# Edge gathers without a loop and with four steps of rows, and sixteen experts without a loop and with five homes of raw weights

## The chip, the cores and the metric

The kernel runs on one core of one Trainium2 chip. The metric is the time of one execution on the device in microseconds (us), the median of three runs. A core has a matrix engine (TensorE, PE in the profile, with its weight loads as PEld), a vector engine (VectorE, DVE), a scalar engine (ScalarE, ACT), a general engine (GpSimd, POOL) that also issues the indirect transfers, and a queue for plain transfers (SyncE, SP). Each engine works through its own list of instructions in order. They meet at semaphores alone, which every transfer and many instructions raise.

## The reference

One layer of a graph network and one layer of experts, over 1250 nodes of 512 values.

```python
xn   = layernorm(x)                                   # 1250 x 512
msg  = relu(xn[src] + edge_attr @ W_e + b_e)          # 21250 edges, sorted by dst
aggr = segment_sum(msg, dst)
h    = silu(bn(((1 + eps) * xn + aggr) @ W1 + b1))    # 1250 x 1024
x    = x + silu(bn(h @ W2 + b2))
t    = layernorm(x)
aff  = softmax(t @ gate_weight)                       # 1250 x 16
gating, index = top_k(aff.T, 156)                     # 156 tokens for each of 16 experts
for e in range(16):
    h = gelu(t[index[e]] @ w1[e] + b1[e])             # 512 x 512 weights
    y = h @ w2[e] + b2[e]
    out[index[e]] += gating[e] * y
out = x + out
```

## The kernel before, in words

Products run in fp16 with each fp32 operand split into a high and a low part, so a product is three matmuls (high by high, high by low, low by high).

**Edges.** The 21250 edges are 34 steps of 5 groups (`J = 5`) of 125 edges. POOL fetches for each group the 125 rows of `node_rows` that `src` names, by one indirect transfer (L413). The rows of a step stand in one of two halves of `rows`, a ring of two steps. Ahead of every second step POOL copies the indices of two steps into `src_now` (L403) and waits for that copy, and ahead of each transfer it waits until PE (`msg_ps`), or for the middle group `Z = 2` DVE (`rowsz_used`), has used the row that stood in its place. PE multiplies the edge attributes (L1165, L1167), adds the fetched rows by two matmuls with a scaled identity (L1182, L1184), and sums the messages of the step before into windows of nodes (L1158). ACT takes the relu (L541) and DVE its low part (L845). For the middle group DVE adds row and product itself (L841). Each engine runs through `run_steps`: a loop of eight turns of four steps, then two steps.

**Middle.** The two node products, their normalisations, the layer norm, the logits, a search for the 156th affinity of each expert (L1000 to L1013), and the places of the chosen tokens (`slot`).

**Experts.** For each expert DVE compares slots (`choose`, ten instructions, L1041), PE turns that into token numbers and gates (`pick_tokens`, L1332), DVE writes `idx` (`indices`, L1056), and POOL gathers 2 x 78 rows of `token_rows` (L426). PE turns the rows (`turn_rows`, L1345), multiplies by w1 (`up`, two halves) and w2 (`down`), both L1202, and turns the result back (`turn_back`, L1380). DVE and ACT weigh it (`weigh`, L1076, L673), and POOL adds the rows to `out` by indirect transfers (L435), each expert's after the last one's have landed (`scatter_end`). The fp32 weights of an expert, 2 x 1024 KB, are loaded by SP into `raw[b]`, two homes, when DVE has finished the low part (L930) of the expert that stood there; ACT makes the high part (L579). Within expert e the engines also work ahead: `pick_tokens`, `indices` and `gather` of expert e+2, `choose` of e+3. PE's order is

```python
up(e, 0); turn_back(e-1); up(e, 1); pick_tokens(e+2); turn_rows(e+1); down(e)
```

DVE's is `expert_low(e+1, 0)`, `weigh(e-1)`, `low_h(e)` (both halves), `columns(e+1)`, `indices(e+2)`, `expert_low(e+1, 1)`, `choose(e+3)`, and POOL's is `scatter(e-1)`, `gather(e+2)`, `scatter_end(e-1)`. The experts run as one, then a loop of three turns of four, then three.

Of the kernel before, what the change touches and what calls it, by code (L numbers as in the profile page):

```python
# [18 lines left out]
def gnn_ffn_kernel(nc, x, src, dst, edge_attr, W_e, b_e, W1, b1, g1, beta1, W2, b2, g2, beta2, eps,  # L19
# [31 lines left out]
    CREDIT = 3 * JP  # L51
# [16 lines left out]
    with ExitStack() as ctx:  # L68
# [12 lines left out]

        def rank(j):

            return j - (j > Z)


        xs = sb("xs", [P, NT, H], F32)
# [9 lines left out]
        We32 = sb("We32", [128, H], F32)  # L97
        We_hi = sb("We_hi", [128, H], F16)
        We_lo = sb("We_lo", [128, H], F16)
        be = sb("be", [P, H], F32)  # L100
        edge = [sb(f"edge{b}", [P, J, ED], F32) for b in range(2)]
        edge_hl = [sb(f"edge_hl{b}", [P, J, 2, ED], F16) for b in range(2)]
        edge_T = [sb(f"edge_T{b}", [128, J, 128], F16) for b in range(2)]
        onehot = [sb(f"onehot{b}", [P, J, WIN], F16) for b in range(2)]
        rel = [sb(f"rel{b}", [P, J], F32) for b in range(2)]
        src_i = sb("src_i", [P, SB, J], I32)
        src_now = [sb(f"src_now{i}", [P, 2, J], I32) for i in range(3)]
        dst_f = sb("dst_f", [P, SB, J], F32)
        dst_left = sb("dst_left", [P, SB, J], F32)
        outside = sb("outside", [P, SB, J], F32)  # L110
# [66 lines left out]
        idx = [sb(f"idx{b}", [KH, 2], U32) for b in range(4)]  # L177
        gat = [sb(f"gat{b}", [KH, 2], F32) for b in range(4)]
# [7 lines left out]
        rows = big[0:P, 0:half].bitcast(F16).rearrange("p (s w h) -> p s w h", w=2, h=H)  # L186
        msg = big[0:P, half:2 * half].bitcast(F16).rearrange("p (s w h) -> p s w h", w=2, h=H)
        rows32 = [big[0:P, (b * J + Z) * H:(b * J + Z + 1) * H] for b in range(2)]
# [10 lines left out]
        pick, xg, xT, hT, h32, yT, yw = [], [], [], [], [], [], []  # L199
        for b in range(2):  # L200
            pick.append(take(P, NT * K // 2).bitcast(F16).rearrange("p (t k) -> p t k", t=NT))
            xg.append(take(KH, 2 * H).bitcast(F16).rearrange("p (a h) -> p a h", a=2))
            xT.append(take(128, HK * K).bitcast(F16).rearrange("p (w k c) -> p w k c", w=2, k=HK))
            hT.append(take(128, HK * K).bitcast(F16).rearrange("p (w k c) -> p w k c", w=2, k=HK))
            h32.append(take(128, HK * K).rearrange("p (k c) -> p k c", k=HK))
        for b in range(2):
            yT.append(z2T[:, b, 0:HK * K].rearrange("p (k c) -> p k c", k=HK))
            yw.append(z2T[0:KH, 2 + b, 0:2 * H].rearrange("p (a h) -> p a h", a=2))
        assert NT == 2 * J and o <= 4 * J * H and HK * K <= N and 2 * H <= N
# [14 lines left out]
        e_raw = [raw[b][:] for b in range(2)]  # L224
# [11 lines left out]

        b1c, g1c, be1c = (colA[:, i * F1:(i + 1) * F1] for i in range(3))
# [8 lines left out]
        xt_ps = sem("xt_ps"); xt_sb = sem("xt_sb"); eps_ready = sem("eps_ready"); pad_clear = sem("pad_clear")  # L246
# [5 lines left out]
        row_in = [sem(f"row_in{i}") for i in range(2 * J)]  # L252
        edge_hi = sem("edge_hi"); edge_lo = sem("edge_lo"); edge_tr = sem("edge_tr"); edge_cp = sem("edge_cp")
        msg_ps = sem("msg_ps"); prod_z = sem("prod_z"); sumz = sem("sumz"); rowsz_used = sem("rowsz_used"); tab32_out = sem("tab32_out"); msg_hi = sem("msg_hi"); msg_lo = sem("msg_lo"); folded = sem("folded")
        rel_ready = sem("rel_ready"); hot_ready = sem("hot_ready"); acc_done = sem("acc_done")
        src_ready = sem("src_ready"); pool_turn = sem("pool_turn"); agg_ready = sem("agg_ready")
# [10 lines left out]
        taken_ps = sem("taken_ps"); slot_ready = sem("slot_ready")  # L267
        pick_ready = sem("pick_ready"); pick_ps = sem("pick_ps"); idx_ready = sem("idx_ready")
        xg_in = [sem(f"xg_in{b}") for b in range(2)]
        ew_in = [[sem(f"ew_in{b}{m}") for m in range(2)] for b in range(2)]  # L270
# [13 lines left out]
        def _(sp):  # L284
# [56 lines left out]
            for b, split in ((0, W1_lo), (1, W2_lo)):  # L341
                sp.wait_ge(split, HK if b == 0 else F1)
                for m, w in enumerate((fw1_t, fw2_t)):
                    sp.dma_start(e_raw[b][:, m, :].rearrange("p (k f) -> p k f", k=HK), w[b]
                                 ).then_inc(ew_in[b][m], 16)
# [5 lines left out]
            for g in range(NT // XG):  # L351
                sp.wait_ge(x16_lo, (g + 1) * XG)
                for r0, r1 in SPRAY:
                    sp.dma_start(rows16_t(token_rows)[r0:r1, g * XG:(g + 1) * XG, :],
                                 x16[r0:r1, g * XG:(g + 1) * XG, :, :].rearrange("p t w h -> p t (w h)")
                                 ).then_inc(rows_out, 16)

            with sp.Fori(0, EX // 2 - 1) as q:
                for b in range(2):
                    for m, w in enumerate((fw1_t, fw2_t)):  # L360
                        sp.wait_ge(e_lo, (q * 2 + b) * 2 + (m + 1))
                        sp.dma_start(e_raw[b][:, m, :].rearrange("p (k f) -> p k f", k=HK),
                                     w[bass.ds(q * 2 + (b + 2), 1)].rearrange("a p k f -> (a p) k f")
                                     ).then_inc(ew_in[b][m], 16)
# [3 lines left out]
        def _(pool):  # L368
# [27 lines left out]
            def step(w, g, b, place):  # L396
                n = w * SB + (g * 2 + b)
                if b == 0:

                    pool.wait_ge(msg_ps, n * JP + JP)  # L400
                    pool.wait_ge(rowsz_used, n + 1)
# [3 lines left out]
                for j in range(J):  # L405
                    if j == Z:
                        pool.wait_ge(rowsz_used, n + 2)
                    else:
                        pool.wait_ge(msg_ps, n * JP + JP + rank(j) + 1)
                    pool.sem_inc(pool_turn, 1)  # L410
                    to, table = (rows32[b], node_rows32) if j == Z else (
                        rows[:, b * J + j, :, :].rearrange("p w h -> p (w h)"), node_rows)
                    pool.indirect_dma_start(to, None, table,  # L413
                                            bass.IndirectOffsetOnAxis(src_now[place][:, b, j:j + 1], 0)
                                            ).then_inc(row_in[b * J + j], 16)

            run_steps(pool, n_pass, SB, step)

            def gather(e):
                b = e[1] % 2  # L420
                pool.wait_ge(idx_ready, num(e) + 1)
                if num(e, least=0) >= 2:
                    pool.wait_ge(xT_ps, num(e) * 2 - 2)
                pool.sem_inc(pool_turn, 1)
                for a in range(2):
                    pool.indirect_dma_start(xg[b][:, a, :], None, token_rows,  # L426
# [12 lines left out]
            def scatter_end(e):  # L439

                pool.wait_ge(y_out[e[1] % 2], pair(e) * 32 + 32)
                pool.sem_inc(scattered, 1)
# [1019 lines left out]
```

## Time and profile before

| what | value |
|---|---|
| median of three runs | 761.31 us (760.77 to 762.72) |
| profiled execution, its own time | 758.0 us |
| its span, from first to last instruction | 756.2 us |
| mean granted TensorE clock | 0.888 of full speed |
| busy: PE, PEld | 530.1, 382.1 us |
| busy: DVE, ACT, POOL | 478.9, 357.5, 360.1 us |
| moved by transfers | 111.34 MB, mean 147 GB/s |

Busy time counts an engine as at work, whatever it waited for in between. The same mean hides stages with different limits, so the stages have to be read one by one: up to 52 us the tables of rows, to 331 us the edges, to 541 us the middle, to 742 us the experts, then the last scatter.

### The profile page before, as it was taken

Reading aid. Unit: us, or ns where it says so; the run is one execution under the profiler, and the core shown is the slowest. Engines: PE = TensorE matmul, PEld = TensorE weight load, DVE = VectorE, ACT = ScalarE, POOL = GpSimd, SP = SyncE. Lnnn points to the kernel's source line nnn. Section 1 sums busy time; section 2 is a strip of 40 time slices with the busy share of each in tenths; the row PEclk is TensorE's granted clock in tenths of the full one; section 3 lists DMA queues with packets and bytes.
Section 4 is the critical chain, followed back from the end, with each engine's and each line's share of the span. In section 5 each row is a group of like instructions: output and inputs, shape, how many; then the busy total and the mean of one; then the engine's idle time right before and its main releaser. Section 6 shows DMA issues by size and latency. Waiting matters only on the chain.

```text
span 756.2 us, 15773 instructions
## 1 busy us (share of the span) xinstructions
PE 530.1 (70%) x5273; PEld 382.1 (51%) x5273; DVE 478.9 (63%) x1042; ACT 357.5 (47%) x610; POOL 360.1 (48%) x284
## 2 busy tenths in 40 slices
PE   1527868788787777769988995712577866968791
PEld 1314445454454444445544554511577866958781
DVE  4944657586666666666539657777566665857650
ACT  0603545355444445454437406530267656756661
POOL 1717777777777777740000000130266456545552
PEclk9999989899989999999998997755589878889996
DMA  7376787868777686643300004150358678688632
GB/s 182 120 215 190 196 197 183 203 180 200 197 182 201 175 203 175 172 115 113 112 0 1 1 0 136 56 182 11 90 148 259 170 212 225 173 218 212 200 52 34
DMA packets 79647, 111.34 MB, mean 147 GB/s; under 512 B 32207, under 2 KB 40842, under 8 KB 79615
## 3 DMA queue, kind: packets, MB, share of 16 engines
q0 software_dynamic: 43712, 53.95, 29.6%
q1 hardware_dynamic: 34637, 56.16, 25.2%
q10 hardware_dynamic: 1266, 0.81, 0.5%
q8 instruction: 19, 0.31, 0.2%
q14 instruction: 13, 0.11, 0.0%
HBM read 95.35 MB, written 15.35 MB: 146 GB/s over the span
## 4 chain that ended last, share of the span: by engine, by line
PE 28%; DMA 19%; issue 17%; POOL 16%; DVE 11%; ACT 5%; POOLq 1%; SPq 0%; ACTq 0%; DVEq 0%
PE bank L1202 16%; POOL big L413 11%; DMA big<-node_rows,src_now 9%; DMA big<-token_rows,idx 6%; POOL out L435 3%; PE bank L1218 2%; POOL big L426 2%; PE bank L1182 2%; DVE stats L699 2%; DMA pair<-in_src 1%; DMA out<-rows_z,idx 1%; PE bank L1345 1%; DVE rows_z L710 1%; PE bank L1184 1%; ACT pair L579 1%
## 5 line engine op out<-in xcount | busy, mean ns | idle before, releaser
L413 POOL DMA_INDIRECT big<-node_rows,src_now x170 | 211.2, 1242 | 63.6 <-issue 43.8
L1202 PE MATMUL bank<-big,pair 128*128 128x156 f16 (+2 forms) x1824 | 177.3, 261 | 7.2 <-DVE big L912 5.3
L1202 PEld LDWEIGHTS bank<-big,pair 128*128 128x128 f16 x1824 | 147.9, 104 | 32.9 <-issue 6.7
L541 ACT ACTIVATE big<-bank 125x512 f16<-125x512 f32 x136 | 81.2, 597 | 127.1 <-PE bank L1184 126.6
L845 DVE SCALAR_TENSOR_TENSOR big<-bank,big 125x512 f16<-125x512 f32 x136 | 90.3, 686 | 41.8 <-ACT big L541 39.0
L1182 PE MATMUL bank<-big,ident_scaled 125*125 125x512 f16 x136 | 59.3, 436 | 71.4 <-DMA big<-node_rows,src_now 70.6
L435 POOL DMA_INDIRECT out<-rows_z,idx x32 | 60.0, 1874 | 61.1 <-ACT rows_z L673 38.2
L426 POOL DMA_INDIRECT big<-token_rows,idx x32 | 55.6, 1738 | 68.3 <-DVE idx L1056 51.9
L454 POOL TENSOR_TENSOR big<-aggT,big 125x512 f16<-125x512 f32 x10 | 11.3, 1155 | 159.3 <-ACT big L602 159.3
L1158 PEld LDWEIGHTS bank<-onehot,big 125*128 125x128 f16 x1400 | 62.5, 101 | 31.9 <-issue 7.5
L1182 PEld LDWEIGHTS bank<-big,ident_scaled 125*125 125x125 f16 x136 | 19.0, 140 | 117.3 <-DMA big<-node_rows,src_now 113.6
L930 DVE SCALAR_TENSOR_TENSOR pair<-raw,pair 128x2048 f16<-128x2048 f32 x32 | 72.9, 2279 | 0.0
L1165 PE MATMUL bank<-We_hi,edge_T 128*125 128x512 f16 x170 | 70.4, 414 | 1.5 <-ACT edge_T L519 1.5
L1167 PE MATMUL bank<-We_lo,edge_T 128*125 128x512 f16 x170 | 67.2, 395 | 0.0
L1158 PE MATMUL bank<-onehot,big 125*128 125x64 f16 x1400 | 66.0, 197 | 1.3 <-DVE big L845 1.3
L579 ACT ACTIVATE pair<-raw 128x2048 f16<-128x2048 f32 x32 | 60.9, 1905 | 0.2
L841 DVE SCALAR_TENSOR_TENSOR big<-big,bank 125x512 f32<-125x512 f32 x34 | 23.3, 686 | 55.6 <-DMA big<-node_rows,src_now 55.6
L1184 PE MATMUL bank<-big,ident_scaled 125*125 125x512 f16 x136 | 54.6, 401 | 0.0
L634 ACT ACTIVATE big<-bank 128x624 f16<-128x624 f16 x16 | 11.1, 692 | 88.1 <-PE bank L1345 87.8
L1345 PE MATMUL bank<-ident,big 78*128 78x78 f16 x256 | 15.5, 232 | 45.4 <-DMA big<-token_rows,idx 45.4
L1345 PEld LDWEIGHTS bank<-ident,big 78*128 78x128 f16 x256 | 13.2, 119 | 46.6 <-DMA big<-token_rows,idx 46.6
L1202 PE MATMUL bank<-rows_z,pair 128*128 128x418 f16 (+1 forms) x192 | 33.9, 338 | 0.0
(197 smaller groups left out, 864.5 us busy)
## 6 DMA issues: line engine op xcount, KB each, us to landing
raw<-in_L_ffn_w SPq DMA_DIRECT2D x32, 1024.0 KB, 6.4
edge<-in_edge_attr SPq DMA_DIRECT2D x35, 140.0 KB
node_rows<-big SPq DMA_DIRECT2D x10, 448.0 KB
raw<-in_L_gnn_W SPq DMA_DIRECT2D x16, 256.0 KB, 7.2
big<-node_rows,src_now POOLq DMA_INDIRECT x170, 5.9
xs<-in_x SPq DMA_DIRECT2D x5, 448.0 KB
out<-xs SPq DMA_DIRECT2D x5, 448.0 KB
token_rows<-big SPq DMA_DIRECT2D x5, 448.0 KB
```

The costliest lines, as they stand in the source:

```text
L413: pool.indirect_dma_start(to, None, table, bass.IndirectOffsetOnAxis(src_now[place][:, b, j:j + 1], 0)).then_inc(row_in[b * J + j], 16)
L426: pool.indirect_dma_start(xg[b][:, a, :], None, token_rows, bass.IndirectOffsetOnAxis(idx[e[1] % 4][:, a:a + 1], 0)).then_inc(xg_in[b], 16)
L435: pool.indirect_dma_start(out, bass.IndirectOffsetOnAxis(idx[e[1] % 4][:, a:a + 1], 0), yw[e[1] % 2][:, a, :], None, compute_op=ALU.add).t ...
L541: act.activation(msg[:, b * J + j, 0, :], rows32[b] if j == Z else bank[j][0:P, :], ACT.Relu).then_inc(msg_hi, 1)
L579: act.activation(pair16[b][:, 0, m, :], raw[b][:, m, :], ACT.Copy, scale=W_SCALE).then_inc(e_hi, 1)
L845: dve.scalar_tensor_tensor(out=msg[:, b * J + j, 1, :], in0=rows32[b] if j == Z else bank[j][0:P, :], scalar=0.0, in1=msg[:, b * J + j, 0, ...
L930: dve.scalar_tensor_tensor(out=pair16[b][:, 1, m, :], in0=raw[b][:, m, :], scalar=W_SCALE, in1=pair16[b][:, 0, m, :], op0=ALU.mult, op1=AL ...
L1158: last = pe.matmul(bank[6 + b][:, k * WIN:(k + 1) * WIN], msg[:, b * J + j, p, k * 128:(k + 1) * 128], onehot[b][:, j, :], start=(j == p = ...
L1165: pe.matmul(bank[j][0:P, :], edge_T[b][:, j, 0:P], We_hi[:], start=True, stop=False, skip_group_check=True)
L1167: return pe.matmul(bank[j][0:P, :], edge_T[b][:, j, 0:P], We_lo[:], start=False, stop=(j == Z), skip_group_check=True)
L1182: pe.matmul(bank[j][0:P, :], ident_scaled[0:P, 0:P], rows[:, b * J + j, 0, :], start=False, stop=False, skip_group_check=True)
L1202: last = pe.matmul(bk, weights(i, k), values(j, k), start=(begin and p == k == 0), stop=(end and p == 2 and k == n - 1), skip_group_check= ...
```

## The change

The edge gathers become straight code, 34 steps with fixed places, a ring of four steps (two in `rows`, two in the room of `pair16`, idle until then), indices read straight from `src_i`, and one pair of waits for each step instead of one for each transfer. Groups 0 and 1 share a semaphore, and so do 3 and 4; the waits for them want both rows. The transposes of the edge attributes move from group 3 to group 1, their copy from group 4 to group 3. The experts become straight code on all engines, with `idx` and `gat` kept for all sixteen, four homes of gathered rows, three of weighed results, and five of raw weights: two as before, and `edge_home`, `xs_home` and `aggT`, which are free at different times. SP loads experts 0, 2, 1 and 5 before the layer's output is stored, 3 and 4 around the storing of the tokens, and the rest as homes come free. `pick_tokens`, `indices` and `gather` work three experts ahead, `choose` four.

```diff
+    RING = 4
+    CREDIT = RING * JP
+    XR = 4
+    YR = 3
+    RH = 5
...
+        def trio(j):
+            return (j >= Z) + (j > Z)
+        def rows_landed(w, g, r, place, n):
+            return w * (16 * n * (SB // RING + (r < SB % RING))) + (g * (8 * n) + n * (16 - 8 * (place % 2)))
...
+        late_rows = [pair16[i][0:P].rearrange("p w a (s h) -> p (w a s) h", h=H)
+                     .rearrange("p (s w) h -> p s w h", w=2) for i in range(2)]
+        def row(r, j):
+            return rows[:, r * J + j, :, :] if r < 2 else late_rows[r - 2][:, j, :, :]
...
+            sp.wait_ge(W1_lo, HK)
+            for m in range(2):
+                load_expert(0, m)
+            sp.wait_ge(agg_ready, 1)
+            for m in range(2):
+                load_expert(2, m)
+            sp.wait_ge(W2_lo, F1)
+            for m in range(2):
+                load_expert(1, m)
+            reload(5)
...
+            for t in range(0, 4, XG):
+                store_tokens(t, XG)
+            sp.wait_ge(x2_out, 16 * NT)
+            sp.wait_ge(xn2_ready, NT)
+            for m in range(2):
+                load_expert(3, m)
+            for t in range(4, NT, XG):
+                store_tokens(t, XG)
+            sp.wait_ge(xt2_ps, NT)
+            for m in range(2):
+                load_expert(4, m)
+            for e in range(6, EX):
+                reload(e)
...
-                    pool.tensor_copy(src_now[place][:], src_i[:, bass.ds(g * 2, 2), :]).then_inc(src_ready, 1)
-                    pool.wait_ge(src_ready, w * (SB // 2) + g + 1)
...
+            with pool.Fori(0, n_pass) as w:
+                for i in range(SB):
+                    ago = RING if i >= SB % RING else SB % RING
+                    pool.wait_ge(msg_ps, w * (SB * JP) + (CREDIT + (i - ago + 1) * JP))
+                    pool.wait_ge(rowsz_used, w * SB + (RING + i - ago + 1))
+                    pool.sem_inc(pool_turn, 1)
+                    for j in range(J):
+                        pool.indirect_dma_start(row32(i % RING) if j == Z else
+                                                row(i % RING, j).rearrange("p w h -> p (w h)"), None,
+                                                node_rows32 if j == Z else node_rows,
+                                                bass.IndirectOffsetOnAxis(src_i[:, i, j:j + 1], 0)
+                                                ).then_inc(row_in[i % RING][trio(j)], 16)
...
+            for e in range(XR - 1):
+                gather(e)
+            for e in range(EX):
+                if e + XR - 1 < EX:
+                    gather(e + XR - 1)
+                if e >= 2:
+                    scatter_end(e - 2)
+                if e >= 1:
+                    scatter(e - 1)
...
+                if e + 1 < EX:
+                    expert_low(e + 1, 0)
+                if e + 3 < EX:
+                    indices(e + 3)
+                low_h(e, 0)
+                if e >= 1:
+                    weigh(e - 1)
+                if e + 1 < EX:
+                    expert_low(e + 1, 1)
+                low_h(e, 1)
+                if e + 1 < EX:
+                    columns(e + 1)
+                if e + 4 < EX:
+                    choose(e + 4)
...
+                pe.wait_ge(idx_ready, min(e + 3, EX))
...
+                up(e, 0)
+                if e + 3 < EX:
+                    pick_tokens(e + 3)
+                if e >= 1:
+                    turn_back(e - 1)
+                up(e, 1)
+                if e + 1 < EX:
+                    turn_rows(e + 1)
+                down(e)
```

## Rows read from the trace of the kernel before

**Rows 1.** Busy us (instructions) by stage: PE, PEld, DVE, ACT, POOL, PEclk, DMA share, GB/s.

```profile
52.00:331.00 279.00, 209.95 (x2091) 126.92 (x2091) 177.20 (x364) 132.27 (x233) 215.73 (x186) 0.95 0.74 187
331.00:541.00 210.00, 145.27 (x931) 88.11 (x931) 140.38 (x335) 82.21 (x129) 16.09 (x14) 0.82 0.18 60
541.00:742.00 201.00, 157.20 (x2187) 155.09 (x2184) 125.44 (x266) 127.76 (x221) 107.83 (x58) 0.87 0.69 183
```

**Rows 2.** The page: the chain that ended last, by line, and two of the costliest groups.

```profile
PE bank L1202 16%; POOL big L413 11%; DMA big<-node_rows,src_now 9%; DMA big<-token_rows,idx 6%; POOL out L435 3%; PE bank L1218 2%; POOL big L426 2%; PE bank L1182 2%; DVE stats L699 2%; DMA pair<-in_src 1%; DMA out<-rows_z,idx 1%; PE bank L1345 1%; DVE rows_z L710 1%; PE bank L1184 1%; ACT pair L579 1%
...
L413 POOL DMA_INDIRECT big<-node_rows,src_now x170 | 211.2, 1242 | 63.6 <-issue 43.8
...
L1345 PE MATMUL bank<-ident,big 78*128 78x78 f16 x256 | 15.5, 232 | 45.4 <-DMA big<-token_rows,idx 45.4
```

**Rows 3.** Timeline of POOL among the edge gathers; the copies over the whole run.

```profile
51.31 0.19 POOL L403 COPY src_now<-src_i 125x10 int32 x1 [15.32 <-issue]
52.64 1.42 POOL L413 DMA_INDIRECT big<-node_rows,src_now  x1 [1.14 <-issue]
...
101.59 1.22 POOL L413 DMA_INDIRECT big<-node_rows,src_now  x1 [0.98 <-PE bank L1184]
103.12 1.21 POOL L413 DMA_INDIRECT big<-node_rows,src_now  x1 [0.31 <-issue]
...
L403 POOL COPY src_now<-src_i x17: 190/208/542, 51.3 to 314.6; 125x10 int32 x16, 125x10 int32<-125x10 int32 x1
```

**Rows 4.** Timeline of DVE: the same instruction of two successive edge steps.

```profile
152.01 0.22 DVE L825 TENSOR_SCALAR rel<-dst_f,shift 125x5 f32 x1
...
157.53 0.49 DVE L825 TENSOR_SCALAR rel<-dst_f,shift 125x5 f32 x1
```

**Rows 5.** Timeline of PE over two experts, and the same products in the straight code near the end.

```profile
600.42 0.73 PE L1345 MATMUL bank<-ident,big 78*128 78x78 f16 x16 [0.37 <-DMA big<-token_rows,idx]
600.99 5.09 PE L1202 MATMUL bank<-big,pair 128*128 128x156 f16 x72
605.92 1.04 PE L1380 MATMUL bank<-ident,rows_z 128*78 128x128 f32 x8
608.44 0.88 PE L1332 MATMUL bank<-tok_aff,big 125*78 x20
615.13 1.22 PE L1345 MATMUL bank<-ident,big 78*128 78x78 f16 x16 [5.80 <-DMA big<-token_rows,idx]
616.15 7.45 PE L1202 MATMUL bank<-big,pair 128*128 128x156 f16 x72
...
727.49 5.09 PE L1202 MATMUL bank<-big,pair 128*128 128x156 f16 x72
```

**Rows 6.** Timeline of POOL and of DVE's L930 in the first of these experts.

```profile
600.22 1.51 POOL L435 DMA_INDIRECT out<-rows_z,idx  x1 [5.54 <-ACT rows_z L673]
601.71 2.28 DVE L930 SCALAR_TENSOR_TENSOR pair<-raw,pair 128x2048 f16<-128x2048 f32 x1
602.03 3.31 POOL L435 DMA_INDIRECT out<-rows_z,idx  x1 [0.30 <-DVE idx L1056]
605.61 2.28 DVE L930 SCALAR_TENSOR_TENSOR pair<-raw,pair 128x2048 f16<-128x2048 f32 x1
605.65 3.12 POOL L426 DMA_INDIRECT big<-token_rows,idx  x1 [0.30 <-issue]
...
609.08 0.99 POOL L426 DMA_INDIRECT big<-token_rows,idx  x1 [0.30 <-issue]
```

**Rows 7.** The chain that ended last, in order of time: start us, us, what.

```profile
729.05 6.28 DMA out<-rows_z,idx
...
738.06 4.24 DMA out<-rows_z,idx
...
743.27 1.47 POOL out L435
```

**Rows 8.** Transfers by issue: count, KB each, median us to landing.

```profile
raw<-in_L_ffn_w SPq DMA_DIRECT2D x32, 1024.0 KB, 6.4
```

More of the change, by code:

```diff
@@ L439, in scatter_end @@
             def scatter_end(e):
-                pool.wait_ge(y_out[e[1] % 2], pair(e) * 32 + 32)
+                pool.wait_ge(y_out[e % 2], e // 2 * 32 + 32)
                 pool.sem_inc(scattered, 1)
-            def expert(e, first=False, ahead=3):
-                if not first:
-                    scatter(after(e, -1))
-                if ahead >= 2:
-                    gather(after(e, 2))
-                if not first:
-                    scatter_end(after(e, -1))
             for t in range(NT):
@@ L683, in _ @@
+            act.wait_ge(z2_ps, 3 * HK)
+            expert_high(1, 0)
+            columns(0)
+            for e in range(EX):
+                expert(e)
+            weigh(EX - 1)
         @block.vector
@@ L1094, in _, with low_h @@
[L1094 to L1102 removed]
+            def low_h(e, half):
+                b, f = e % 2, slice(half * 2, half * 2 + 2)
+                dve.wait_ge(h_high, e * 2 + half + 1)
+                dve.tensor_tensor(hT[b][:, 1, f, :], h32[b][:, f, :], hT[b][:, 0, f, :],
+                                  ALU.subtract).then_inc(h_sb, 1)
@@ L1105, in _ @@
+            dve.wait_ge(rows_out, 16 * NT)
+            choose(0)
+            choose(1)
+            for e in range(3):
+                indices(e)
+                if e < 2:
+                    choose(e + 2)
+            columns(0)
+            for e in range(EX):
+                expert(e)
+            weigh(EX - 1)
         @block.tensor
@@ new lines, in down @@
+                pe.wait_ge(e_lo, e * 2 + 2)
+                if e >= 1:
+                    pe.wait_ge(yT_sb, e * HK)
+                for half in range(2):
+                    pe.wait_ge(h_sb, e * 2 + half + 1)
+                    for d in range(HK):
+                        last = product(bank[4 + d // 2][:, d % 2 * K:(d % 2 + 1) * K], 2,
+                                       lambda i, k: e16[b][:, i, 1, half * 2 + k, d * 128:(d + 1) * 128],
+                                       lambda j, k: hT[b][:, j, half * 2 + k, :],
+                                       begin=(half == 0 and d % 2 == 0), end=(half == 1))
+                        if half == 1:
+                            last.then_inc(yT_ps, 1)
@@ L1393, in expert @@
                 down(e)
-            pick_tokens((0, 0))
-            pick_tokens((0, 1))
-            turn_rows((0, 0))
-            run_experts(pe, expert)
-            turn_back((0, EX - 1))
-def num(e, least=None):
-    q, c = e
-    if least is not None and not isinstance(q, int):
-        return 4 * least + c
-    return q * 4 + c
-def pair(e):
-    q, c = e
-    return q * 2 + c // 2
-def after(e, n):
-    return (e[0], e[1] + n)
+            for e in range(3):
+                pick_tokens(e)
@@ L1420, in run_steps @@
+            turn_rows(0)
+            for e in range(EX):
+                expert(e)
+            turn_back(EX - 1)
 def run_steps(eng, n_pass, steps, step, turn=None, turn_end=None):
@@ L1431, in run_steps @@
             step(w, steps // 2 - 1, b, 2)
-def run_experts(eng, expert):
-    expert((0, 0), first=True)
-    with eng.Fori(0, 3) as q:
-        for c in range(1, 5):
-            expert((q, c))
-    expert((0, 13), ahead=2)
-    expert((0, 14), ahead=1)
-    expert((0, 15), ahead=0)
 def kernel(**inputs):
```

402 lines of the change are left out of this document (168 added, 234 removed).

## The prediction

> **What bounds the kernel now.** I read the chain that ended last first. Apart from PE's products it names POOL's edge gathers, 11%, and the landing of two kinds of gathered rows, 9% and 6% [rows 2]. No engine is full on average, so I cut the span into stages [rows 1]. There are three: the edges, 279 us, with POOL busiest (215.7 us); the middle, 210 us, with transfers at a share of 0.18; and the experts, 201 us, with PE busiest at 157.2 us and its granted clock down at 0.87.
>
> The timeline of POOL shows that it sets the pace of the edges. An edge gather takes 1.24 us on average [rows 2], the next starts 0.30 us later, and that gap does not grow where a semaphore has to be awaited [rows 3]. So 170 gathers want 170 x 1.242 + 169 x 0.305 = 262.7 us, and the stage takes some 278 (52.6 to 331). What is left is the copy of indices. The other engines keep up: DVE begins successive steps 5.5 us apart where the rows are there [rows 4], against 5 x 1.55 = 7.7 us that POOL needs for a step. PE's waits for gathered rows in this stage are POOL's pace seen from behind.
>
> In the experts PE runs one expert in 8.9 us when nothing is late: it starts to turn rows at 600.42 and ends picking at 608.44 + 0.88 = 609.32 [rows 5]. Then it waits 5.80 us for the next gathered rows, and after that wait the same 72 products take 7.45 instead of 5.09 us [rows 5]. Such waits sum to 45.4 us over the run [rows 2]. A row of this stage thus has two costs, the wait and the slow products behind it. The stage's mean is 201/16 = 12.6 us an expert [rows 1].
>
> **The change part by part, edges.** (a) The first copy goes: the copy starts at 51.31, the first gather at 52.64 [rows 3], so -1.3 us. (b) Each of 16 later copies (median 0.21 us) stands with its wait of 0.98 us where otherwise 0.30 us stand [rows 3]: 16 x 0.89 = -14.2. These are POOL's own time, and POOL is the pace, so they come off whole. (c) The ring of four costs or gains nothing in the sum: POOL waits no longer for a place now. It would only pay if the landing time were the pace. The waits moved to the step's head, the later rows in `pair16` and the moved transposes are covered by the 2.2 us a step in which PE and DVE wait for POOL; without that cover, a step is 5.5 us, still below 7.7. (d) The shared semaphores let PE begin group 3 only when group 4 has landed. Within the stage the 2.2 us cover it; at the end one more group of a step comes after the last landing, 5.5/5 = +1.1. Edges together: -14.4.
>
> **Middle.** The loads of experts 2, 5, 3 and 4, 8 MB, run where the transfers' share is 0.18 [rows 1]; a piece of 1 MB lands in 6.4 us [rows 8], and the stage is 210 us long. So 0. If a load stood before the storing of tokens for long, the gather of expert 0 would be late; there are tens of us of search between, so I keep nothing of it. Two more `choose` and a third `pick_tokens` before the first rows are turned: the gather of expert 0 lands meanwhile, but its descriptors are made while DVE is busier. An operation of POOL can stretch from 1.5 to 3.3 us there [rows 6]; between 0 and +2 I take +1.
>
> **Experts.** Gathers are issued two experts or more before PE turns their rows, some 15 us and more against one of 9 us now, so the 5.8 us wait goes, and the slow products with it. What is late next? The bounds of an expert's period:
>
> - Below: PE's 8.9 us [rows 5]. DVE's and ACT's busy time, 125.4/16 = 7.8 and 127.8/16 = 8.0 us [rows 1], leave it room, though `low_h(e, 1)` now stands behind a 2.28 us L930, which can hold `down` for about 0.5 us.
> - Above: POOL. The four transfers of an expert took 600.22 to 610.07 = 9.85 us in one go, two of them stretched from 1.5 and 1.0 to 3.3 and 3.1 us. Each stretched one starts while L930 runs and ends 1 to 1.4 us after it [rows 6]. L930 runs twice per expert, near half of a shorter period, so a third can be hit: 9.85 + 1.8 = 11.6 us. The chain of scatters gives the same size: an issue with its gap, 1.8 or 3.6, a landing of 6.3 and a wake of 1.0 make 9.1 to 10.9 us [rows 7].
>
> I take 9.8 us, the measured POOL sequence, since it is the one resource that already shows this length. With 2 us for the last turning back and weighing the stage is 16 x 9.8 + 2 = 159 against 201: -42. The five homes give their part only here: with two, a period of 9.8 would have to hold two loads and two conversions of the same home; with five, a load has some four periods against 2 x 6.4 us [rows 8].
>
> The row says that POOL stalls behind L930. The Trainium skill, "SBUF — State Buffer", section "Who interferes with whom", says that a DVE instruction with two SBUF inputs contends with a GpSimd instruction that reads SBUF, and that the loser blocks fully; L930 reads `raw` and `pair16`, and the trace agrees (3.31 against 1.51 us). By that rule every transfer that starts inside L930 loses the rest of its 2.28 us, and all four hit would make 6.2 + 4 x 2 = 14 us an expert; it speaks against counting on PE's 8.9.
>
> **Tail.** At the end scatter stands behind scatter: the last begins at 743.27, after the landing of the one before, and 13 us remain from it to the end of the span [rows 7]. That stays. POOL may now be part of an expert behind PE when PE ends, between 0 and 5 us; I take +2.
>
> **Sum.** -14.4 + 0 + 1 - 42 + 2 = -53.4 us from the profiled execution's 758.0 (span 756.2, 1.8 around it): 704.6. The median of the runs is 3.3 above that execution, so 708.
>
> **Rivals.**
>
> - *POOL and the scatters set 11.6 us.* For it: L930 stretches transfers [rows 6], and gathers, scatters and their landing follow each other in POOL's list. Against: two of four transfers were hit, not three. Experts 16 x 11.6 + 2 = 188, 29 us more than forecast: 737.
> - *PE sets 8.9 us.* For it: a whole expert ran so [rows 5]. Against: POOL's 9.85. 14 us less: 694, and with no lag at the end 691.
> - *The edges gain nothing*, because the landing or DVE's wait for the middle row, not POOL's issue, is the pace. Against: the gaps of 0.30 [rows 3]. Experts as forecast: 708 + 15 = 723.
> - *The wait for rows stays*, since `indices` of the third expert ahead, POOL's list or full transfer queues make gathers as late as now. A period of 9.8 moves 2.74 MB (two weight pieces and four times 78 rows of 2 KB), 280 GB/s, against 183/0.69 = 265 at full share [rows 1]. For it: ten experts' loads then fill the queues. Against: four homes in hand. Only the edges gain: 761 - 14 = 747. The Trainium skill, "SBUF — State Buffer", section "A bandwidth-pool intuition that's wrong", gives 358 GB/s between HBM and a core, by which the queues would not fill; 265 is what I reckon with.
> - *Slower: the engines wait for their own instructions.* Without loops each expert's code is new. If PE lost a landing of 6.4 us [rows 8] per expert on that, the period is 8.9 + 6.4 = 15.3, the stage 247, the time 761 - 11 + 46 = 796. It decides from (201 - 2 + 11)/16 = 13.1 us, that is from 4.2 us an expert. Against: the last three experts are straight code already, and their 72 products take the same 5.09 us [rows 5].
>
> **How the numbers follow.** Forecast, a period of 9.3 to 10.5 us (700 to 720): 0.50. POOL near 11.6: 0.17. PE near 8.9: 0.15. Edges without gain: 0.10. Wait for rows stays: 0.05. Slower: 0.03. The range runs from the PE case, 691, to just short of 11.6 us, 734; it leaves out most of the last two cases and the outer half of the POOL case. Within 0.3%, 2.3 us, a measurement of this kernel can tell nothing; the cases put 0.01 there, 0.96 on faster and 0.03 on slower.
>
> **What the profile after would show.** Edges: no copy, one gather each 1.55 us without a break, the stage some 263 us long. Experts: no wait of PE for `token_rows` after the first; a period near 9.8 us with POOL nearly gapless, its transfers of 3 us beside L930; clock above 0.87. Loads of six experts before 541 us. The prediction is wrong if PE's wait for rows is still there, if POOL's gap in the edges was something else than the copy, or if POOL's transfers stretch further than two in four.

## The result, and the profile after

The changed kernel took 736.44 us (median of 4, 733.0 to 738.94) against 761.22 us of the kernel before (760.77 to 762.72): a ratio of 0.967, 95% interval 0.962 to 0.972. That is a gain of 25 us, somewhat less than half of the 53 forecast, and the time lies outside the range of 691 to 734 us. The profiled execution took 733.0 us, its span is 731.2 us.

I cut its span as before: at 331 us, where the edges ended then, and where PE first turns gathered rows and ends its last turning back. In the windows view the columns are those of [rows 1].

```profile
52.00:331.00 279.00, 215.77 (x2102) 142.28 (x2103) 178.19 (x365) 129.41 (x233) 209.16 (x170) 0.93 0.79 190
331.00:538.00 207.00, 144.64 (x940) 88.42 (x937) 141.59 (x346) 82.12 (x128) 16.14 (x15) 0.83 0.26 89
538.00:704.00 166.00, 145.74 (x2175) 141.78 (x2172) 122.93 (x253) 126.33 (x221) 120.94 (x54) 0.97 0.68 181
704.00:731.00 27.00, 0.00 (x0) 0.00 (x0) 0.28 (x1) 0.63 (x1) 8.78 (x6) 0.55 0.29 36
```

The comparison below goes by events instead, since the edges end elsewhere now. They come from PE's instructions by line (count, ns min/median/max, first and last start in us): the first product of z1, the turning of gathered rows, the turning back.

```profile
L1265 PE MATMUL bank<-rows_z,pair x96: 337/340/555, 338.7 to 356.8; 128*128 128x418 f16 x96
...
L1387 PE MATMUL bank<-ident,big x256: 196/201/267, 537.5 to 689.7; 78*128 78x78 f16 x128
...
L1422 PE MATMUL bank<-ident,rows_z x128: 270/273/308, 551.3 to 703.6; 128*78 128x128 f32 x128
```

In the kernel before the first starts of the first two and the last start of the third read 341.0, 539.9 and 741.1 us. So the edges and the middle gave 2.4 us (forecast 13.4), the experts 201.2 - 166.1 = 35.1 (forecast 42), and the tail, from there to the end of the span, took back 27.6 - 15.1 = 12.5 (forecast 2). The sum is the 25.0 us by which the spans differ. Two things need a cause: edges almost without gain, and a long tail behind experts that gained 7 us less than forecast.

**Edges.** The copies are gone: POOL's timeline shows gather after gather with 0.30 us between them, over most step ends too, and the last starts at 317.4 instead of 329.7 us. But the first product of z1 comes 21 us behind it, where 11 us stood before. The list of waits for 60 to 320 us says who is slow (us in total, times, longest):

```profile
ACT big L588 <- PE bank L1231: 61.6, 57, 7.3
DVE big L892 <- ACT big L588: 51.9, 45, 3.4
ACT big L588 <- remote: 37.5, 27, 2.3
...
PEld bank L1189 <- DVE edge_home L883: 22.9, 12, 2.5
```

PE's waits for rows, 60.1 us in the same window of the kernel before, are down to 14 us. ACT waits for PE, DVE for ACT, and PE for DVE at the transposes (L1189). For "remote" the trace has no work that ends then. The timeline shows what is late: PE's second matmul with the identity (L1231) raises the semaphore that ACT's relu of the same bank (L588) waits for.

```profile
148.49 0.38 PE L1231 MATMUL bank<-pair,ident_scaled 125*125 125x512 f16 x1
...
152.40 0.60 ACT L588 ACTIVATE big<-bank 125x512 f16<-125x512 f32 x1 [1.68 <-remote]
```

The matmul ends at 148.87, ACT has been idle for 1.68 us, and the relu starts at 152.40: 3.5 us late. The trace's record of the semaphore has the raise at 152.30, just ahead of the relu and 3.4 us behind the end of the matmul. In the kernel before, the 136 relus of this kind start 0.11 to 0.20 us behind the end of their matmul. The work of PE is done, but the word of it, the raise, comes late. I call words late or prompt by this from here on.

**Tail.** The list of waits of the experts names gathered rows with 14.6 us in 7 waits; the 45.4 us of [rows 2] have shrunk, not gone. The chain in order of time shows where it runs instead (start, us): through the landings of scatters. The first four take 9 to 12 us, where [rows 7] had 4.2 and 6.3 near the end.

```profile
560.05 9.04 DMA out<-rows_z,idx
572.09 10.96 DMA out<-rows_z,idx
586.35 10.61 DMA out<-rows_z,idx
599.79 11.94 DMA out<-rows_z,idx
```

And when PE ends at 703.8, POOL has three experts still to add, 7.0 us apart (the first of the two scatters of each):

```profile
704.34 1.47 POOL L482 DMA_INDIRECT out<-rows_z,idx  x1 [3.61 <-DVE rows_z L1120]
...
711.32 1.47 POOL L482 DMA_INDIRECT out<-rows_z,idx  x1 [3.75 <-DMA out<-rows_z,idx]
...
718.30 1.47 POOL L482 DMA_INDIRECT out<-rows_z,idx  x1 [3.75 <-DMA out<-rows_z,idx]
```

The two groups of the experts' transfers on the page (busy, mean ns, idle before): a scatter takes 1.5 us where it is alone, a gather 1.0, and both means are well above.

```profile
L482 POOL DMA_INDIRECT out<-rows_z,idx x32 | 77.7, 2427 | 39.1 <-issue 18.0
...
L473 POOL DMA_INDIRECT big<-token_rows,idx x32 | 56.9, 1779 | 49.0 <-DVE idx L1101 40.1
```

### The profile page after: what moved, and what is told of

Its sections match the earlier page's. It is cut to its first block, busy times and chain, and to the rows that moved or that the text cites. A ratio compares the mean times of both kernels' runs of the same rounds, so it can differ in the third digit from the quotient of the medians.

```text
span 731.2 us, 14739 instructions
## 1 busy us (share of the span) xinstructions
PE 523.9 (72%) x5273; PEld 384.5 (53%) x5273; DVE 478.9 (65%) x1042; ACT 353.7 (48%) x610; POOL 372.5 (51%) x267
## 4 chain that ended last, share of the span: by engine, by line
PE 42%; DMA 15%; issue 13%; DVE 12%; POOL 8%; ACT 5%; another core or an unknown queue 3%; DVEq 0%; SPq 0%; POOLq 0%; ACTq 0%
PE bank L1249 14%; DMA out<-rows_z,idx 9%; PE bank L1205 5%; PE bank L1212 5%; PE bank L1231 4%; PE bank L1214 4%; POOL out L482 4%; PE bank L1229 3%; PE bank L1265 3%; POOL big L473 2%; DMA pair<-in_src 2%; DVE stats L747 2%; PE bank L1189 1%; ACT big L588 1%
## 5 line engine op out<-in xcount | busy, mean ns | idle before, releaser
L588 ACT ACTIVATE big<-bank 125x512 f16<-125x512 f32 x136 | 80.3, 596 | 124.3 <-PE bank L1231 65.9
L461 POOL DMA_INDIRECT big<-node_rows,edge_home x90 | 110.8, 1231 | 45.5 <-issue 39.6
L461 POOL DMA_INDIRECT pair<-node_rows,edge_home x80 | 98.4, 1230 | 26.8 <-issue 21.6
L482 POOL DMA_INDIRECT out<-rows_z,idx x32 | 77.7, 2427 | 39.1 <-issue 18.0
L1205 PEld LDWEIGHTS bank<-edge_home,big 125*128 125x128 f16 x1400 | 68.5, 102 | 39.3 <-issue 15.9
L1205 PE MATMUL bank<-edge_home,big 125*128 125x64 f16 x1400 | 76.6, 199 | 5.3 <-issue 3.4
L1212 PE MATMUL bank<-edge_home 128*125 128x512 f16 x170 | 73.8, 434 | 6.5 <-issue 2.6
L1214 PE MATMUL bank<-edge_home 128*125 128x512 f16 x170 | 69.1, 407 | 1.3 <-issue 1.2
L1189 PE MATMUL bank<-ident,edge_home 125*128 125x125 f16 x175 | 16.8, 231 | 42.6 <-DVE edge_home L883 21.1
L1229 PE MATMUL bank<-big,ident_scaled 125*125 125x512 f16 x72 | 29.8, 414 | 9.8 <-DMA big<-node_rows,edge_home 9.5
L1189 PEld LDWEIGHTS bank<-ident,edge_home 125*128 125x128 f16 x175 | 10.5, 102 | 46.7 <-DVE edge_home L883 22.9
L977 DVE SCALAR_TENSOR_TENSOR pair<-raw,pair 128x2048 f16<-128x2048 f32 x14 | 31.8, 2281 | 2.8 <-ACT pair L626 2.0
L1212 PEld LDWEIGHTS bank<-edge_home 128*125 128x125 f16 x170 | 24.7, 145 | 11.7 <-ACT edge_home L580 3.4
L1229 PE MATMUL bank<-pair,ident_scaled 125*125 125x512 f16 x64 | 27.1, 424 | 4.8 <-DMA pair<-node_rows,edge_home 4.6
L930 DVE BATCH_NORM_STATS2 st<-big 128x6 f32<-128x418 f32 (+1 forms) x24 | 14.1, 592 | 25.1 <-ACT big L608 25.1
```

What stands on the lines that cost most here:

```text
L461: pool.indirect_dma_start(row32(i % RING) if j == Z else row(i % RING, j).rearrange("p w h -> p (w h)"), None, node_rows32 if j == Z else ...
L482: pool.indirect_dma_start(out, bass.IndirectOffsetOnAxis(idx[:, e, a:a + 1], 0), yw[e % YR][:, a, :], None, compute_op=ALU.add).then_inc(y ...
L588: act.activation(msg[:, b * J + j, 0, :], row32(r) if j == Z else bank[j][0:P, :], ACT.Relu).then_inc(msg_hi, 1)
L977: dve.scalar_tensor_tensor(out=pair16[e % 2][:, 1, m, :], in0=e_raw[e % RH][:, m, :], scalar=W_SCALE, in1=pair16[e % 2][:, 0, m, :], op0=A ...
L1189: last = pe.transpose(bank[5][:].bitcast(F16)[:, j * 128:j * 128 + P], edge_hl[b][:, j, :, :].rearrange("p a c -> p (a c)"), ident16[0:P, ...
L1205: last = pe.matmul(bank[6 + b][:, k * WIN:(k + 1) * WIN], msg[:, b * J + j, p, k * 128:(k + 1) * 128], onehot[b][:, j, :], start=(j == p = ...
```

## Experiments on the edges

Theories: A, the gathers of a step stand back to back with no instruction on a semaphore between them, and this delays the word of other engines; B, the transposes, moved to group 1, wait there for DVE. Further rivals, which the expectation of the first run names, are late rows or shared semaphores (C) and full transfer queues (D).

**Raise ahead of each gather; transposes back; both; raises in the experts too.**

```diff
-                    pool.sem_inc(pool_turn, 1)
                     for j in range(J):
+                        pool.sem_inc(pool_turn, 1)
```

```diff
-                    if j == 1:
+                    if j == 3:
                         edge_transposes(n + 1, 1 - b)
```

(with ACT's copy ahead of group 4 instead of 3)

> One raise of a semaphore that nothing waits for stands ahead of each edge gather again (170 in all, instead of 34). Theory A: POOL's gathers, back to back with no instruction on a semaphore between them, hold up the word that PE's matmuls give to ACT; the relus then start 0.1 us after their matmul as in the kernel before, a step falls from 8.4 to 7.8 us and the end of the edges comes some 10 us earlier: 736 - 10 = 726 us. Rivals B (the transposes moved to group 1), C (late rows or shared semaphores) and D (the transfer queues are full): the raise costs POOL at most some 0.05 us each, no change, 735 to 745 us.

> The transposes of the edge attributes stand behind group 3 again, their copy before group 4. Theory B: PE stood 2.1 us a step at the moved transposes, waiting for DVE's low part of the attributes; with them back the wait is covered and the edges end up to 10 us earlier: 726 us. Theory A (POOL's back-to-back gathers delay the semaphores): the wait moves elsewhere and the step stays at 8.4 us: 735 to 740 us, or somewhat slower.

> Both edits: a raise ahead of each edge gather and the transposes back behind group 3. If each had a part of the loss the two add up here: A alone 726, B alone 726, both with a part 722 to 726; if neither (late rows, shared semaphores or full queues set the step), 735 to 740 us.

> A raise ahead of each edge gather as in the first run, and also between the two transfers of every gather and scatter of the experts. Against the first run: if the word of PE, ACT and DVE is held up in the experts as well while POOL issues, an expert falls below 10.2 us and the time is 3 to 8 us below that of the first run; if POOL's transfers, stretched by the copies of the weights, or the transfer queues set the period, no difference (within 1 us).

Measured: 721.27 (ratio to the kernel before on that chip 0.950, interval 0.945 to 0.955), 715.49 (0.938, 0.931 to 0.945), 718.36 (0.944, 0.938 to 0.950) and 724.59 us (0.951, 0.944 to 0.958). Each edit alone gave the whole gain, z1's first product at 324.0, 327.4 and 322.9 us, and the relus start 0.12 us behind their matmul in all four (0.32 at most). That fits neither theory, which each wanted its own edit; the changed kernel had not been run beside them. The raises in the experts gained nothing that can be told from the spread of the runs.

**The changed kernel again.**

> The changed kernel unaltered, beside the others on one chip. If the slow edges belong to the program (ACT's relus up to 5 us behind their matmul, steps of 8.4 us), the time is 733 to 739 us again and the relus lag again; if they are a state that comes by chance, some executions come near 720 us, as the runs with one of the two edits did.

730.24 us (725.36 to 738.5, the last the profiled one), z1 at 339.7, relus up to 4.9 us late. But three kernels beside it on that chip, which hold both edits (next section), had late relus too and z1 at 335.5 to 337.2. So the edits do not cure it, and A and B fall as its cause. They may soften it: there the relus are 0.9 to 1.0 us late on the mean, in the three profiles of the changed kernel with late words 1.75 to 1.8.

**Before, changed, and both edits on a third chip.**

> The kernel before, unaltered, profiled on the same chip as the next two. If the delay between PE's word and ACT's relu belongs to the chip, it shows here too when it shows in the changed kernel; if it belongs to the gathers without an instruction on a semaphore between them, the relus start 0.1 us after their matmul here whatever the others do.

> The changed kernel a third time. Delay of the program: relus late, 730 to 739 us, last relu near 334 us. Delay of the chip: on a chip without it the last relu is near 320 us and the time near 720 us, with no difference to the next run.

> A raise ahead of each edge gather and the transposes back, as in the third run. Delay of the program: against the changed kernel on this chip 10 us or more faster, relus not late. Delay of the chip: the same as the changed kernel within 4 us, late or not late as it is.

761.18, 721.33 (ratio 0.947, 0.943 to 0.952) and 726.51 us (0.951, 0.944 to 0.958). Here the changed kernel with no edit is as fast as with them, and C and D, which it holds unaltered, fall too. At the place shown above its relu is prompt:

```profile
149.51 0.38 PE L1231 MATMUL bank<-pair,ident_scaled 125*125 125x512 f16 x1
...
150.01 0.60 ACT L588 ACTIVATE big<-bank 125x512 f16<-125x512 f32 x1 [0.53 <-PE bank L1231]
```

and PE waits for rows again, as forecast (60 to 320 us):

```profile
ACT big L588 <- PE bank L1231: 120.8, 129, 7.8
DVE big L892 <- ACT big L588: 49.7, 61, 3.2
PEld bank L1229 <- DMA big<-node_rows,edge_home: 44.1, 27, 10.0
```

**Before and changed side by side, twice.**

> The kernel before beside the changed one on the same chip. If late relus are a matter of the chip alone, they show here whenever they show in the next run. If the chip only opens the way and the gathers without an instruction on a semaphore between them bring it about, the relus start 0.1 us after their matmul here even where those of the next run are late.

> The changed kernel beside it. Relus at once: about 720 us, last relu near 321 us. Relus late: 725 to 739 us, last relu near 334 us.

759.0 and 725.5 us, relus prompt in both. Then once more:

> The kernel before beside the changed one. Chip alone: relus late here whenever they are late in the next run. Chip and gathers together: relus at once here even where the next run has them late.

> The changed kernel beside it. Relus at once: 718 to 726 us. Relus late: 725 to 739 us.

772.07 and 734.93 us, relus late in both. In this profile of the kernel before the matmul ends at 177.47 and the relu starts 1.40 us later:

```profile
177.09 0.38 PE L1184 MATMUL bank<-big,ident_scaled 125*125 125x512 f16 x1
...
178.87 0.59 ACT L541 ACTIVATE big<-bank 125x512 f16<-125x512 f32 x1
```

Its first z1 product comes at 352.6 instead of 338.5 to 341.0. This pair ran on the chip on which the first four runs were prompt. So late words come in either kernel and are not bound to one chip. They cost the kernel before 12 to 14 us up to z1 and the changed one 13 to 18 (338.7 to 342.8 against 324.5 and 325.6). Whether the change has a part in how often they come is open. The unaltered changed kernel has them in 3 of 5 profiles, the kernel before in 1 of 4. In the session of 730.24 us the seven executions of the kernel before took 757.2 to 767.9 us, like prompt ones, while all four kernels profiled in it had late words; the result itself was such a pair. Compared like with like the change gains 38.0 us (spans 757.2 and 719.2), 33.5 (757.2 and 723.7), and with late words in both 37.3 (770.3 and 733.0). The first comparison, with its 25 us, set a kernel before with prompt relus against a changed one with late relus.

## Experiments on the experts

Theories: F, the loads of weights fill the transfer queues, so that scatters land late; S, DVE's low part of the weights (L977) stretches POOL's transfers. For S this piece of the changed kernel's timeline speaks, as [rows 6] did. The scatter of 5.12 us begins 0.5 us ahead of an L977 and ends 2.3 us behind its end; the one of 3.80 us begins 0.3 us behind the start of an L977 and ends 1.8 us behind its end. The gather at 605.21, 0.2 us ahead of the next L977, keeps its 1.01 us.

```profile
597.98 1.50 POOL L482 DMA_INDIRECT out<-rows_z,idx  x1 [1.87 <-issue]
599.79 5.12 POOL L482 DMA_INDIRECT out<-rows_z,idx  x1 [0.30 <-issue]
605.21 1.01 POOL L473 DMA_INDIRECT big<-token_rows,idx  x1 [0.30 <-issue]
...
612.74 3.80 POOL L482 DMA_INDIRECT out<-rows_z,idx  x1 [4.15 <-DVE rows_z L1120]
```

```profile
600.31 2.28 DVE L977 SCALAR_TENSOR_TENSOR pair<-edge_home,pair 128x2048 f16<-128x2048 f32 x1
602.51 0.47 DVE L1112 TENSOR_TENSOR big<-big 128x312 f16<-128x312 f32 x1
602.90 0.47 DVE L1106 COPY big<-bank 128x624 f16<-128x624 f16 x1
603.29 1.79 DVE L1089 TENSOR_SCALAR big<-iota_slot,slot 125x156 f16<-125x156 f16 x10
...
605.44 2.29 DVE L977 SCALAR_TENSOR_TENSOR pair<-xs_home,pair 128x2048 f16<-128x2048 f32 x1 [0.36 <-ACT pair L626]
...
612.47 2.28 DVE L977 SCALAR_TENSOR_TENSOR pair<-xs_home,pair 128x2048 f16<-128x2048 f32 x1
614.67 0.47 DVE L1112 TENSOR_TENSOR big<-big 128x312 f16<-128x312 f32 x1
```

The rest of this trace is alike. Of the 64 transfers of the experts 28 are under way when an L977 ends. The gathers among them end 0.8 to 1.4 us behind it, the scatters 1.35 to 1.9 and once 2.3, whenever they began; that is about what a transfer takes alone. So a hit transfer gets on only when that DVE instruction is over, and its length depends on when L977 starts beside it.

**Without loads, without the low part, without scatters.** On the kernel with both edits of the edges; all three ran with late words, as the changed kernel beside them (730.24 us).

```diff
-            for e in range(6, EX):
-                reload(e)
```

```diff
+                part = slice(0, 64) if e else slice(0, HK * H)
-    ... out=pair16[e % 2][:, 1, m, :], in0=e_raw[e % RH][:, m, :]
+    ... out=pair16[e % 2][:, 1, m, part], in0=e_raw[e % RH][:, m, part]
```

```diff
-                    pool.indirect_dma_start(out, ... yw[e % YR][:, a, :] ...)
```

> Both edits of the edges, and the weights of experts 6 to 15 are not loaded (old weights are used again; 20 MB less to move). Theory F (the loads fill the transfer queues; scatters and gathers land late, the chain of scatters takes 12 to 15 us an expert while loads run and PE is stopped by it): PE keeps 9.2 us an expert, the stage is 16 x 9.2 + 3 = 150 us instead of 170, and the tail is shorter: 690 to 697 us. Theory S (transfers are stretched from 1.5 to 4 us by DVE's work, queues do not matter): 710 to 718 us.

> Both edits of the edges, and DVE's low part of the expert weights is made for 64 of 2048 columns only (left out: the rest of the low part of experts 1 to 15). Theory S: scatters and gathers take 1.5 and 1.0 us instead of up to 4.4, the chain of scatters is below 9 us and PE keeps 9.2: 690 to 700 us. Theory F (full queues): 712 to 718 us, with the landings as slow as before and little changed but DVE's busy time.

> Both edits of the edges, and the experts' rows are weighed but not added to the output (all 32 scatters left out). If the chain of scatters is what stops PE, every expert takes PE's 9.2 us, the stage 150 us, and the tail of 24 us falls to 3: 673 to 680 us. If late gathers (full queues) stop PE by themselves, waits for token rows of 10 us and more remain and the stage stays above 158 us: 683 us or more.

| | us | turn rows to turn back | tail | mean scatter, gather |
|---|---|---|---|---|
| changed, same chip | 730.24 | 538.7 to 708.5 | 28.2 | 2.48, 1.79 |
| no loads | 728.21 | 536.2 to 696.2 | 28.1 | 2.58, 1.84 |
| low part a stub | 698.99 | 534.5 to 678.1 | 19.1 | 1.55, 1.06 |
| no scatters | 694.37 | 534.2 to 684.6 | 6.3 | -, 1.94 |

The times are medians; the stages are read from the profiles, and that of the changed kernel is its slowest execution, 738.5 us. F falls as the main cause: 20 MB less moved, and the time is the same within the spread (718.6 to 733.4 against 725.4 to 738.5), the stage at most 10 us shorter. S stands: with the stub the scatters take 1.46 to 2.13 us and the gathers 0.96 to 1.75. The runs with the stub and without scatters are 31 and 36 us below the changed kernel, and either lets PE run at its own pace nearly throughout (waits for rows of 2.7 us in all). The stage's 144 us with the stub are 9.0 an expert. The stub also takes two pieces of 2.28 us an expert out of DVE's own list, ahead of `low_h` and `weigh`, so its 31 us are not POOL's share alone; no run parts the two. The first scatter to the last (first and last start of L482, less 1.8 us, over 15) is the chain's period: 11.0 us in the changed kernel on this chip (10.7 in the first profile), 10.2 without loads, 8.7 with the stub. Its links can stand in for each other: with loads the landings of scatters are 43% of the chain between 540 and 660 us, without them 4%, and there POOL's own scatters and gathers take 38 and 23%, for a period only 0.8 us shorter.

**Low part in halves; halves alone; quarters.** The pieces stand apart, with `indices`, `low_h`, `weigh` and `columns` between them.

```diff
+                for p in parts:
+                    c = slice(p * HK * H // 2, (p + 1) * HK * H // 2)
+                    last = dve.scalar_tensor_tensor(out=pair16[e % 2][:, 1, m, c], ...)
...
-                    expert_low(e + 1, 0)
+                    expert_low(e + 1, 0, (0,))
...
+                    expert_low(e + 1, 0, (1,))
```

> Both edits of the edges, and DVE makes each low part of the weights in two halves with other work between them (four pieces of 1.15 us an expert instead of two of 2.28). If a transfer waits only for the one DVE instruction that it meets, it loses at most 1.15 us: mean scatter 1.9 us or less (2.3 to 2.5 now), the chain of scatters 9.5 us instead of 10.7, time 8 to 16 us below the run before this one. If POOL loses whatever DVE's low part takes in sum, the mean scatter stays at 2.3 us or above and the time within 4 us.

> The changed kernel with the low part of the weights in two halves as the one edit. From the run with both edits and halves (705 us against 726 without halves on that chip, 721 for the changed kernel): 701 to 708 us where relus are not late, 712 to 720 where they are. If the gain of halves hung on the edge edits, 718 us or more.

> The low part in four quarters (eight pieces of some 0.6 us an expert), spread further. If a transfer loses what is left of the one DVE instruction that it meets, mean scatter falls from 1.87 (halves) to 1.7 us and the time 3 to 6 us below halves. If POOL gets in between two pieces only where DVE pauses, no gain over halves: within 3 us, or worse by the fixed cost of more instructions.

With both edits of the edges 705.19 us (ratio 0.926, 0.921 to 0.931) against 726.51 without halves; alone 703.46 (0.923, 0.914 to 0.932) against 725.5 of the changed kernel's one run there; quarters 705.82 (0.926, 0.918 to 0.935). Halves beat both kernels; quarters add nothing. POOL's two groups in the changed kernel and then with halves alone, on one chip:

```profile
L482 POOL DMA_INDIRECT out<-rows_z,idx x32 | 83.4, 2606 | 45.3 <-issue 16.8 <-DVE rows_z L1120 15.8 <-DMA out<-rows_z,idx 11.3
L473 POOL DMA_INDIRECT big<-token_rows,idx x32 | 51.7, 1615 | 49.1 <-DVE idx L1101 40.9 <-issue 7.6 <-DVE rows_z L1120 0.3
```

```profile
L473 POOL DMA_INDIRECT big<-token_rows,idx x32 | 65.4, 2045 | 48.5 <-DVE idx L1105 40.3 <-issue 8.2
L482 POOL DMA_INDIRECT out<-rows_z,idx x32 | 59.6, 1864 | 34.1 <-issue 15.4 <-DMA out<-rows_z,idx 15.1 <-ACT rows_z L701 3.4
```

POOL's sum per expert falls only from 8.4 to 7.8 us, against 5.2 with the stub. A transfer that gets past one piece can meet the next: one gather of the run with halves took 6.63 us over four pieces, which is why shorter pieces alone do not help. But the loss has moved from scatters, which stand in the chain, to gathers, which POOL issues while a scatter lands; the chain's period goes from 11.2 to 9.7 us, and PE's own from 9.2 to 8.8. That `low_h` no longer stands behind a piece of 2.28 us fits this; like the scatters' waits for DVE's weighing, 15.8 us before and 0.2 at most now, it is then a gain of DVE's order and not of POOL's:

```profile
582.13 1.05 PE L1429 MATMUL bank<-ident,rows_z 128*78 128x128 f32 x8
590.89 1.05 PE L1429 MATMUL bank<-ident,rows_z 128*78 128x128 f32 x8
599.65 1.05 PE L1429 MATMUL bank<-ident,rows_z 128*78 128x128 f32 x8
```

## Why the prediction was wrong

The measured gain is 28.4 us short of the forecast by the profiled pair: 11.0 in the edges (late words), 6.9 in the experts and 10.5 in the tail (the chain of scatters). With prompt words the changed kernel's 721.33 and 725.5 us lie inside the range, 13 and 18 us above the forecast; what took the first measurement out of it is the edges' part. Two steps failed: that the copies "come off whole", which holds with prompt words only, and the costing of the chain of scatters.

Here are forecast and measured us, for the two pairs of profiles with prompt words (ahead: 757.2 and 719.2, then 757.2 and 723.7 us of span): edges and middle -13.4 and -11.6, -15.4; experts -42 and -37.4, -31.3; tail +2 and +11.0, +13.2; sum -53.4 and -38.0, -33.5.

- *(a), (b), copies of the indices:* right. The gap that "does not grow where a semaphore has to be awaited" is not among [rows 3], but the trace has it (0.30 us at 109.38, released by PE). The last gather starts 12.3 us earlier, and where words are prompt the gain arrives whole at the middle (mean -13.5 of -13.4).
- *(b), "these are POOL's own time, and POOL is the pace, so they come off whole", and the cover in (c):* right with prompt words. The cover of 2.2 us a step that I counted on is gone when words come late, and PE stands at the moved transposes (21.1 us behind DVE's L883): only 2.4 us arrived instead of 13.4. What makes the words late stays open. My rival of edges without gain blamed the landing or DVE's wait for the middle row, neither of which shows, and the profile before had nothing of late words.
- *Middle:* nothing to correct; loads of six experts hid in it (198.8 us from z1 to the first turning of rows, 198.9 before).
- *Experts, a period of 9.8 us, "the measured POOL sequence":* the step that failed besides the edges. It took one undisturbed sequence of four transfers, two of them stretched, with POOL as the only link. The chain of scatters has landings in it too, mostly 9 to 12 us while loads run against the 6.3 I used, and its period was 10.5 to 11.2 us. The rival of 11.6 us named both links and was nearer in the period, but not in the stage (188 us against 166 to 173 measured and 159 forecast). Its 737 us meets the measured 736.44 by luck, since late words in the edges make up the rest.
- *PE in the experts:* its own period is 9.2 us, not 8.9. The reason given, `low_h` behind L930 (now L977), fits the 8.8 us with halves and with the stub (quarters: 9.1). The wait for rows fell from some 47 to between 14 and 24 us; without scatters 2.7 us are left of it, so the chain of scatters brings it back.
- *Tail, +2:* the largest error next to the edges. I let POOL be part of an expert behind. With three homes of weighed results PE can run three experts ahead, and a chain slower than PE uses all of them: PE pays late, and the debt stands at the end, where the changed kernel has two more pairs of scatters of 7.0 us behind PE. Part of what the experts gained was only moved to the tail: 35 us there, 12.5 taken back.
- *Transfers beside DVE's low part:* "each stretched one starts while L930 runs" was too narrow, since transfers that begin up to 0.6 us ahead are hit as well. Counted, 28 of 64 were hit in the first profile, and POOL's four transfers take 8.2 to 8.5 us of an expert in the five profiles of the changed kernel, against 8.9 in the sequence of [rows 6] that I used. POOL's own part was sized well; the landings between the scatters were not. The stub takes 0.9 us from the mean scatter and 0.7 from the mean gather, 3.3 us an expert. The rule of the Trainium skill, "SBUF — State Buffer", section "Who interferes with whom", by which a DVE instruction with two SBUF inputs contends with a GpSimd instruction that reads SBUF, was weighed as speaking against PE's 8.9 us only; these runs agree with it in kind, with less than the 8 us an expert that I worked out from it.

## What to carry to other kernels

A buffer ring in front of a serial chain does not make the chain faster. It hides its lag until the ring is full or the program ends, so cost the chain by itself, with its landings under the load that the change brings, and put (period of chain - period of producer) times the steps, up to the ring's depth, into the tail. Here three homes of results left two more experts to add behind PE, 14 us. Where a long instruction of one engine stretches another's transfers, cut that instruction and see that its pieces meet the transfers that have slack. And repeat the kernel before beside the changed one on more than one occasion before explaining a difference that no edit controls.

## What the runs showed of the hardware

- In some executions the word of PE reaches ACT late through most of the edge gathers: 65 to 96 of 136 relus start over 0.2 us behind their matmul, on the mean of all 0.9 to 1.8 us, at most 4.1 to 6.5 us. From 3 us behind the start of the last gather on, all are prompt again (0.25 us at most). Up to z1's first product it costs 12 to 18 us. It was there in 7 of 20 profiles of this case, in both kernels. No edit brought or cured it, and one chip showed both. What decides it stays open.
- DVE's scalar_tensor_tensor with two operands in SBUF (128x2048, 2.28 us) holds an indirect transfer of POOL until it ends. In the five profiles of the changed kernel all 86 transfers that began during one ended behind it, and 46 of 64 that began up to 0.6 us ahead of one; scatters of 1.5 us became 3.8 to 5.1 us where they met it near its start. In halves (1.21 us) it costs scatters 0.4 instead of 1.1 us on the mean, and gathers 1.0 instead of 0.6.
- Removing 20 MB of loads took the DMA share between 560 and 640 us from 0.89 to 0.33, and the median by 2 us, less than the runs vary.
